# Placing the weighing of a tile behind the next tile's choice, and feeding the input patterns one tile earlier, in a four-layer graph and feed-forward kernel

## The chip, the cores and the metric

The kernel runs on one core of one Trainium2 chip, as one launch. The metric is the device time of a run in microseconds (us), from its start to its end; lower is better. The profiler's span of an execution is nearly that time (1441.6 us of 1443.37 us here).

## The reference

Four layers work on 1250 tokens of width 512, in fp32: a three-step graph network, a mixture of 16 experts with three chosen per token, a graph layer with attention and batch normalization, and the layer that this case is about, with the residual x added to each:

```
h           = layernorm(x)                                    # 1250 x 512
input_acts  = gelu(h @ input_patterns.T)                      # 1250 x 256
proc        = gelu(input_acts @ process_input_weights.T)      # 1250 x 1024
top, idx    = top_k(proc, 128)
agg         = softmax(top) @ process_values[idx]              # 1250 x 256
output_acts = gelu(agg @ output_input_weights.T)              # 1250 x 256
x           = x + output_acts @ output_patterns
```

So each token keeps the 128 largest of its 1024 process activations, weighs them by a softmax, and mixes the values with these weights.

## The kernel before

The 1250 tokens are ten tiles of 125 (`NT = 10`). Every engine has one program with its instructions in fixed order. Semaphores order the engines against each other, and an instruction that waits holds everything behind it on its engine. The layers before the last one are not touched by the diff.

**Inputs of the last layer.** VectorE normalizes tile i (line 449), TensorE turns it with four transposes (`pe_turn`, line 454) into one of two banks, and ScalarE copies it to SBUF (`act_turned`, line 460, which raises `hT_in`). `pe_inputs(c, f)` multiplies the pair of tiles 2c and 2c+1 with half f of the input patterns: eight records of 250 columns at line 426. It waits until both tiles of its pair are copied. There are five pairs and two halves, so ten such groups. In the loop, the group for pair and half `divmod(i - 2, 2)` follows the turn of tile i, so the turn of one more tile stands between a pair's last turn and its first group. Behind the loop stand the two groups of the last pair. ScalarE then loads its Gelu table and evicts six pieces (line 1015), and TensorE begins the process products when all six are there.

**The choice.** A threshold per token is refined by counts, so that a little over or just under 128 values stay above it. GpSimd marks what lies below the threshold (line 734) and leaves the rest in `rest` (line 736). For tile i it does so when tile i-2 is chosen (`bad_ready`). VectorE then finds the exact cut in `vec_choose(i)`: eight largest of the rest (line 1285), replace them (lines 1286 and 1289), the next eight (line 1292), a small subtraction (line 1297), and small instructions on 16 or 1 columns (lines 1300 to 1309), whose last raises `bad_ready`. TensorE adds up the flags of `bad` over the partitions (line 2264) and ScalarE stores the sum as an integer (line 810, which raises `bad_in`).

**The weighing.** `vec_weigh(i)` waits for that integer and for the exponentials, reads the integer into a register (`value_load`, line 1315), branches, and in the usual branch does one `scalar_tensor_tensor` over 1024 columns with two SBUF inputs (line 1327), which keeps the exponentials of the chosen values and sums them. Its end raises `weighed`. A reciprocal of the sum follows (line 1330, raising `w_inv_ready`). TensorE turns the weights with eight transposes (line 2249), ScalarE copies them, TensorE multiplies them with the values in 16 records (line 426), ScalarE applies Gelu, and TensorE multiplies with the output patterns. VectorE adds the result to x (line 1757), and SyncE stores it.

**The order of the last loop.** The choices of tiles 0 and 1 (`EARLY = 2`) and their weighings stand ahead of it, between the refinements. In the loop over t from 2 to 14, VectorE first adds the finished tile t-5 and then makes the choice of tile t. The weighing of tile t-1 is called inside that choice, right behind line 1292. Tile 9's weighing stands behind the add of tile 5. TensorE's iteration t turns the weights of tile t-3, turns the outputs of t-4, sums the flags of t-2, multiplies the patterns of t-5 and the values of t-3, in this order.

Of the kernel before, what the change touches and what calls it, by code (L numbers as in the profile page):

```python
# [17 lines left out]
NT = N_TOK // TP  # L18
# [3 lines left out]
IN_PAIRS = 5  # L22
# [40 lines left out]
EARLY, EARLY_FROM, CHOICE_PARTS = 2, 5, 4  # L63
# [17 lines left out]
def build(nc, a):  # L81
    with ExitStack() as ctx:
# [3 lines left out]
        def sem(name):  # L86
            return ctx.enter_context(nc.semaphore(name))
# [176 lines left out]
        def expert_views(slot):  # L264
# [150 lines left out]
        weighed, w_inv_ready, w_turned, wT_in, pv_mm, pv_in = (  # L415
            sem(n) for n in ("weighed", "w_inv_ready", "w_turned", "wT_in", "pv_mm", "pv_in"))
# [7 lines left out]
        def group(e, out, pairs):  # L424
            for n, (l, r) in enumerate(pairs):
                ins = e.matmul(out, l, r, start=(n == 0), stop=(n == len(pairs) - 1))  # L426
            return ins
# [56 lines left out]
        def of_tiles(t, s, first=0, last=NT):  # L484

            return [first + t - s] if 0 <= t - s < last - first else []
# [790 lines left out]
            e.wait_ge(v_own, v.n)  # L1277
            e.scalar_tensor_tensor(thr[:, c], left[:, c], step[:, c], thr[:, c], ALU.mult, ALU.add).then_inc(done, 1)

        def vec_choose(e, i, part, weigh=None):  # L1280

            c, r = slice(i, i + 1), rest[:, i % 2, :]
            if part == 0:
                e.wait_ge(chosen_pool, BELOW + 2 * i + 1)
                e.max(cand[:, i, 1:9], r).then_inc(v_own, v.up())
                e.tensor_copy(cand[:, i, 0:1], thr[:, c]).then_inc(v_own, v.up())
                e.wait_ge(v_own, v.n)
            elif part == 1:
                e.match_replace(r, cand[:, i, 1:9], r, REPLACED).then_inc(v_own, v.up())
                e.wait_ge(v_own, v.n)  # L1290
            elif part == 2:
                e.max(cand[:, i, 9:17], r).then_inc(v_own, v.up())

                if weigh is not None:
                    vec_weigh(e, weigh)
                e.wait_ge(counted_c, i + 1)
                e.tensor_scalar(left[:, c], cnt[:, c], float(K_PROC - N_PROC), None, ALU.add).then_inc(v_own, v.up())
                e.wait_ge(v_own, v.n)
            else:
                e.scalar_tensor_tensor(cut_junk, iota16, left[:, c], cand[:, i, 0:16], ALU.is_equal, ALU.mult,  # L1300
                                       accum_out=cut[:, c]).then_inc(v_own, v.up())
                e.wait_ge(v_own, v.n)
                e.tensor_scalar(cut_junk, cand[:, i, 1:17], cut[:, c], None, ALU.is_ge, ALU.add,
                                accum_out=cut_cnt[:, c]).then_inc(v_own, v.up())
                e.tensor_scalar(bad[:, c], cut[:, c], 0.0, None, ALU.is_le).then_inc(v_own, v.up())
                e.wait_ge(v_own, v.n)
                e.tensor_tensor(cut_cnt[:, c], cut_cnt[:, c], left[:, c], ALU.not_equal).then_inc(v_own, v.up())
                e.wait_ge(v_own, v.n)
                e.tensor_tensor(bad[:, c], bad[:, c], cut_cnt[:, c], ALU.add).then_inc(bad_ready, 1)

        def vec_weigh(e, i):
            r, w = junk[:, 1, :], wexp[i % 3]
            e.wait_ge(bad_in, i + 1)
            e.wait_ge(exp_ready, i + 1)
            failed = e.value_load(bad_i[0:1, i:i + 1], min_val=0, max_val=2 * TP)
            with e.If(failed > 0):
                src = acts[:, i, :]
                for n in range(K_PROC // 8):
                    e.max(top_s, src)
                    e.drain()  # L1320
                    e.match_replace(r, top_s, src, REPLACED)
                    e.drain()
                    src = r
                e.scalar_tensor_tensor(w, r, REPLACED, w, ALU.is_equal, ALU.mult,
                                       accum_out=w_sum[:, i:i + 1]).then_inc(weighed, 1)
            with e.Else():
                e.scalar_tensor_tensor(w, acts[:, i, :], cut[:, i:i + 1], w, ALU.is_ge, ALU.mult,
                                       accum_out=w_sum[:, i:i + 1]).then_inc(weighed, 1)
            e.wait_ge(weighed, i + 1)
            e.reciprocal(w_inv[:, i:i + 1], w_sum[:, i:i + 1]).then_inc(w_inv_ready, 1)  # L1330
# [13 lines left out]
        def vector(e):  # L1344
# [409 lines left out]
            for t in range(EARLY, NT + 5):  # L1754
                for i in of_tiles(t, 5):
                    e.wait_ge(pat_mm, i + 1)
                    e.tensor_tensor(x_res[:, i, :], x_res[:, i, :], psum[0:TP, 6 + i % 2, :], ALU.add).then_inc(x_last, 1)
                for i in of_tiles(t, 0):
                    for part in range(CHOICE_PARTS):
                        vec_choose(e, i, part, i - 1 if i > EARLY else None)  # L1760
                if t == NT:
                    vec_weigh(e, NT - 1)


        def pe_z(e, l, i, w, b):
# [145 lines left out]
        def pe_busy(e, b, operand, n, rows=128):  # L1911

            for _ in range(n):
                e.matmul(psum[0:rows, b, :], ident[0:rows, 0:rows], operand, start=True, stop=True)  # L1914
# [10 lines left out]
        def pe_inputs(e, c, f):  # L1925

            if c == 0 and f == 0:
                e.wait_ge(ld_last, 16)
                e.wait_ge(pv_in, 4)
            e.wait_ge(hT_in, 5 * NT + 2 * c + 2)  # L1930
            o = c * 2 * TP
            ins = group(e, psum[:, 2 + c // 2 * 2 + f, c % 2 * 2 * TP:(c % 2 + 1) * 2 * TP],
                        [(w_ip[:, k, f * 128:(f + 1) * 128], hT[:, k, o:o + 2 * TP]) for k in range(KD)])
            if c % 2 == 1 or c == IN_PAIRS - 1:
                ins.then_inc(ia_mm, 1)
# [38 lines left out]
        def tensor(e):  # L1974
# [244 lines left out]
            for i in range(NT):  # L2219
                e.wait_ge(ln_out, 3 * NT + i + 1)  # L2220
                if i >= 2:
                    e.wait_ge(hT_in, 5 * NT + i - 1)
                pe_turn(e, htok[:, i, :], i % 2)
                if i >= 2:
                    pe_inputs(e, *divmod(i - 2, 2))
            for f in range(2):
                pe_inputs(e, IN_PAIRS - 1, f)


            for i in range(NT):  # L2230
# [9 lines left out]
            e.wait_ge(pv_in, 4)  # L2240
            for t in range(EARLY, NT + 5):
                for i in of_tiles(t, 3):
                    e.wait_ge(weighed, i + 1)
                    for g in range(2):
                        if i >= 1:
                            e.wait_ge(wT_in, 2 * (i - 1) + g + 1)
                        for k in range(4):
                            c = (4 * g + k) * 128
                            ins = e.transpose(psum[:, 1 + g, k * TP:(k + 1) * TP], wexp[i % 3][:, c:c + 128],
                                              ident[0:TP, 0:TP])  # L2250
                        ins.then_inc(w_turned, 1)
                if t == EARLY + 1:
                    pe_busy(e, 7, w_op[:, 0, :], 2)
                for i in of_tiles(t, 4):
                    e.wait_ge(o_in, i + 1)
                    e.wait_ge(outT_in, i)
                    for k in range(2):
                        ins = e.transpose(psum[:, 4, k * TP:(k + 1) * TP], o_act[:, i % 2, k * 128:(k + 1) * 128],
                                          ident[0:TP, 0:TP])
                    ins.then_inc(o_turned, 1)  # L2260
                for i in of_tiles(t, 2):
                    e.wait_ge(bad_ready, i + 1)
                    e.wait_ge(bad_in, i)
                    e.matmul(psum[0:1, 0, 0:1], ones_col, bad[:, i:i + 1], start=True, stop=True).then_inc(bad_mm, 1)
                if t == EARLY:
                    pe_busy(e, 7, w_op[:, 0, :], 6)

                for i in of_tiles(t, 5):
                    e.wait_ge(outT_in, i + 1)
                    if i >= 2:  # L2270
                        e.wait_ge(x_last, i - 1)
                    group(e, psum[0:TP, 6 + i % 2, :], [(outT[:, i % 2, k, :], w_op[:, k, :])
                                                        for k in range(2)]).then_inc(pat_mm, 1)
                for i in of_tiles(t, 3):
                    e.wait_ge(wT_in, 2 * i + 2)
                    e.wait_ge(o_in, i)
                    group(e, psum[0:TP, 3, 0:D_PV], [(wT[:, i % 2, k, :], w_po[:, k, :])
                                                     for k in range(8)]).then_inc(o_mm, 1)
# [60 lines left out]
```

## Time and profile before

| what | value |
|---|---|
| median of three runs | 1439.91 us (1437.83 to 1443.37) |
| the profiled execution, its own time | 1443.37 us |
| its span | 1441.6 us |
| TensorE matmuls busy | 1311.9 us, 91% |
| VectorE busy | 582.5 us, 40% |
| ScalarE busy | 467.7 us, 32% |
| GpSimd busy | 206.5 us, 14% |
| chain that ended last | PE 76%, DVE 9%, DMA 6%, ACT 3% |

PE is TensorE, DVE is VectorE, ACT is ScalarE, POOL is GpSimd; an engine's name with a q is its sequencer, which runs waits, register loads and branches. The shares are of the whole span. The diff touches two short stages: from about 1280 to 1308 us (normalization and input patterns) and from about 1366 us to the end (choices, weighings, values). So what counts is the order of instructions in these two stretches. Times in the rows are in us from the start of the span.

### The profile page before, as it was taken

To read this page: it belongs to the slowest core of one execution; us is meant where nothing else is said; L and a number is where in the kernel's file an instruction comes from. 1 tells how busy PE (TensorE), PEld (TensorE's weight loads), DVE (VectorE), ACT (ScalarE), POOL (GpSimd) and SP (SyncE) were. 2 spreads that over 40 slices of the span, in tenths; PEclk is the share of its full clock that TensorE was granted. 3 is DMA by queue.
4 is the path that set the end of the run, shared out by engine and by line. 5 is a ranking of instruction groups with operands and counts; after the bars stand their busy time and mean duration, and the time that the engine had idled before them with its cause. 6 is when DMAs were issued, how large, how long until landed. Compare 5 with 4: busy or idle time off the path is not lost.

```text
span 1441.6 us, 18234 instructions
## 1 busy us (share of the span) xinstructions
PE 1311.9 (91%) x5780; PEld 832.3 (58%) x5781; DVE 582.5 (40%) x1558; ACT 467.7 (32%) x1004; POOL 206.5 (14%) x207
## 2 busy tenths in 40 slices
PE   4899999999999899899898999898479999999787
PEld 2454485566466454377575776665355577565465
DVE  9999822111144351111111111111275334675894
ACT  5799632222122200011111111111122333327883
POOL 1000000000000046000101111101383000022361
PEclk9999999999999899999999999999879989999899
DMA  9100000000111214241156115244352000100001
GB/s 219 60 1 1 2 1 0 2 1 1 47 56 33 99 24 148 94 136 44 63 187 217 44 44 207 94 160 167 110 160 94 1 30 1 67 0 1 0 24 50
DMA packets 45297, 96.92 MB, mean 67 GB/s; under 512 B 8495, under 2 KB 10857, under 8 KB 44065
## 3 DMA queue, kind: packets, MB, share of 16 engines
q1 hardware_dynamic: 27205, 68.70, 14.2%
q0 software_dynamic: 10560, 16.23, 4.2%
q10 hardware_dynamic: 7452, 10.97, 2.1%
q8 instruction: 45, 0.74, 0.2%
q14 instruction: 35, 0.29, 0.1%
HBM read 79.72 MB, written 16.10 MB: 66 GB/s over the span
## 4 chain that ended last, share of the span: by engine, by line
PE 76%; DVE 9%; DMA 6%; ACT 3%; issue 3%; ACTq 1%; POOL 1%; DVEq 1%; SPq 0%; POOLq 0%
PE psum L426 38%; PE psum L1802 13%; PE psum L1857 7%; PE psum L1782 4%; PE psum L1997 3%; DMA sb_w_reg<-w_gnn 2%; DMA slot_outs<-sb_blk 2%; PE psum L1914 2%; PE psum L454 2%; PE psum L1940 1%; PE psum L1882 1%; ACT sb_htok L799 1%; DMA sb_blk<-rows,sb_blk 1%; PE psum L1832 1%; PE psum L2212 1%
## 5 line engine op out<-in xcount | busy, mean ns | idle before, releaser
L426 PE MATMUL psum<-sb_w_reg,sb_blk 128*128 128x256 f32 x896 | 206.2, 384 | 1.0 <-issue 1.0
L426 PEld LDWEIGHTS psum<-sb_w_reg,sb_blk 128*128 128x128 f32 x896 | 169.8, 193 | 33.3 <-issue 12.1
L1802 PE MATMUL psum<-sb_z_reg_r,sb_hT_conv_r 125*125 125x512 f32 x400 | 170.9, 427 | 0.2 <-issue 0.2
L426 PE MATMUL psum<-sb_w_reg,sb_hT_conv 128*125 128x512 f32 (+1 forms) x376 | 167.2, 594 | 0.0
L1802 PE MATMUL psum<-sb_htok_r,sb_hT_conv_r 125*125 125x512 f32 x300 | 118.8, 396 | 0.0
L1190 DVE TENSOR_TENSOR sb_blk<-sb_blk,psum 128x256 f32<-128x256 f32 x56 | 23.6, 422 | 221.5 <-ACT sb_blk L773 221.5
L426 PEld LDWEIGHTS psum<-sb_w_reg,sb_hT_conv 128*125 128x125 f32 (+1 forms) x376 | 68.4, 188 | 76.5 <-issue 75.8
L1857 PE MATMUL psum<-sb_w_reg,sb_blk 128*128 128x512 f32 x224 | 108.2, 605 | 2.2
L426 PE MATMUL psum<-sb_hT_conv,sb_w_reg 128*128 128x416 f32 (+3 forms) x336 | 104.7, 469 | 0.0
L752 ACT CAST sb_hT_conv_r<-sb_a_reg 125x625 fp32r<-125x625 f32 x80 | 56.1, 715 | 116.6 <-PE psum L1802 116.5
L1802 PEld LDWEIGHTS psum<-sb_z_reg_r,sb_hT_conv_r 125*125 125x125 f32 x400 | 76.0, 190 | 25.2 <-issue 7.6
L1997 PE MATMUL psum<-sb_hT_conv,sb_sil 125*125 125x400 bf16 x316 | 74.7, 364 | 13.5 <-DVE sb_a_reg L1405 5.3
L426 PEld LDWEIGHTS psum<-sb_hT_conv,sb_w_reg 128*128 128x128 f32 x336 | 64.8, 196 | 35.8 <-issue 32.0
L1397 DVE TENSOR_SCALAR sb_hT_conv<-sb_sil,sb_blk 125x400 bf16<-125x400 f16 x316 | 84.4, 370 | 0.0
L1782 PE MATMUL psum<-sb_w_reg,sb_hT_conv 128*125 128x512 f32 x160 | 81.4, 600 | 3.3 <-DMA sb_w_reg<-w_gnn 3.3
L1997 PEld LDWEIGHTS psum<-sb_hT_conv,sb_sil 125*125 125x125 bf16 x316 | 43.7, 143 | 67.9 <-DVE sb_a_reg L1405 34.9
L862 ACT ACTIVATE sb_blk<-sb_sil,sb_blk 125x125 bf16<-125x125 f16 x237 | 77.2, 391 | 7.1 <-DVE sb_blk L1359 5.6
L773 ACT ACTIVATE sb_blk<-psum 128x256 f32<-128x256 f32 x56 | 21.5, 383 | 168.3 <-PE psum L426 164.3
L426 PE MATMUL psum<-sb_w_reg,sb_z_reg 128*125 128x512 f32 x160 | 69.4, 594 | 1.3 <-ACT sb_z_reg L1015 0.7
L663 POOL IOTA sb_blk<- 125x160 f32 x1 | 0.3, 307 | 465.9 <-DVE sb_blk L1101 465.9
L1802 PEld LDWEIGHTS psum<-sb_htok_r,sb_hT_conv_r 125*125 125x125 f32 x300 | 56.3, 188 | 17.4 <-issue 4.8
L1857 PEld LDWEIGHTS psum<-sb_w_reg,sb_blk 128*128 128x128 f32 x224 | 40.2, 189 | 37.1 <-issue 26.8
(383 smaller groups left out, 1835.9 us busy)
## 6 DMA issues: line engine op xcount, KB each, us to landing
sb_hT_conv<-w_expert SPq DMA_DIRECT2D x7, 2048.0 KB, 11.2
sb_w_reg<-w_expert SPq DMA_DIRECT2D x6, 2048.0 KB, 9.6
sb_hT_conv<-w_expert SPq DMA_DIRECT2D x7, 1024.0 KB, 13.3
slot_outs<-sb_blk ACTq DMA_DIRECT2D x28, 256.0 KB
sb_w_reg<-w_expert SPq DMA_DIRECT2D x6, 1024.0 KB, 12.2
sb_w_reg<-w_gnn SPq DMA_DIRECT2D x1, 4096.0 KB, 44.8
sb_w_reg<-w_qkv SPq DMA_DIRECT2D x1, 3072.0 KB, 18.8
slot_outs<-sb_blk ACTq DMA_DIRECT2D x1, 2560.0 KB, 10.5
```

Of the source, the lines that this page charges most:

```text
L426: ins = e.matmul(out, l, r, start=(n == 0), stop=(n == len(pairs) - 1))
L454: ins = e.transpose(psum[:, b, k * TP:(k + 1) * TP], src[:, k * 128:(k + 1) * 128], ident[0:TP, 0:TP])
L752: e.copy(counts_at(l, n), adj[:, h * HALF_T:(h + 1) * HALF_T, tile(i)]).then_inc(counts_in, 1)
L773: e.activation(silg[:, h, :], psum[:, 1 + h, 0:HF], ACT.Silu).then_inc(s_sil, 1)
L862: e.activation(sq_lo[t % 2][:, j, :], neg_iota, ACT.Square, bias=neg_lo[:, c:c + 1], scale=-1.0).then_inc(lo_squared, 1)
L1190: e.tensor_tensor(hid[:, h * HF:(h + 1) * HF], silg[:, h, :], psum[:, 1 + h, HF:2 * HF], ALU.mult).then_inc(s_hid, 1)
L1397: e.tensor_scalar(hot_key[n][:, j, :], key_iota, key[:, c:c + 1], None, ALU.is_equal).then_inc(hot_ready, 1)
L1782: ins = e.matmul(psum[0:TP, bank, :], hT[:, k, tile(i)], w_gnn[:, 0 if own else 1, k, :], start=(k == 0), stop=(k == KD - 1))
L1802: ins = e.matmul(psum[0:TP, b, :], counts_at(l, 2 * i + n // NT)[:, s % HALF_T, :], z[s], start=(n == 0), stop=(n == len(pairs) - 1))
L1857: ins = e.matmul(psum[:, 5, :], hidT[:, k, :], w_dn[:, k, :], start=(k == 0), stop=(k == KD - 1))
L1914: e.matmul(psum[0:rows, b, :], ident[0:rows, 0:rows], operand, start=True, stop=True)
L1997: ins = e.matmul(psum[0:TP, t % 3, 0:KEYS], hot_lo[n][:, j, :], hot_key[n][:, j, :], start=(j == 0), stop=(j == RUN - 1))
```

## The change

Three edits. In `vec_choose` the call of `vec_weigh` behind line 1292 is taken out, and the last loop calls `vec_weigh(t-1)` behind the whole of `vec_choose(t)`; tile 9's weighing comes at t = 10 in both kernels, behind the add of tile 5. On TensorE, the turning of tile i's weights waits for `w_inv_ready` (the reciprocal) where it waited for `weighed` (the sum). And `pe_inputs` moves up by one tile: the group `divmod(i - 1, 2)` follows the turn of tile i, and one group is left behind the loop where there were two.

```diff
-        def vec_choose(e, i, part, weigh=None):
+        def vec_choose(e, i, part):
...
             elif part == 2:
                 e.max(cand[:, i, 9:17], r).then_inc(v_own, v.up())
-
-                if weigh is not None:
-                    vec_weigh(e, weigh)
                 e.wait_ge(counted_c, i + 1)
...
                 for i in of_tiles(t, 0):
                     for part in range(CHOICE_PARTS):
-                        vec_choose(e, i, part, i - 1 if i > EARLY else None)
-                if t == NT:
-                    vec_weigh(e, NT - 1)
+                        vec_choose(e, i, part)
+                if t > EARLY:
+                    for i in of_tiles(t, 1):
+                        vec_weigh(e, i)
...
                 pe_turn(e, htok[:, i, :], i % 2)
-                if i >= 2:
-                    pe_inputs(e, *divmod(i - 2, 2))
-            for f in range(2):
-                pe_inputs(e, IN_PAIRS - 1, f)
+                if i >= 1:
+                    pe_inputs(e, *divmod(i - 1, 2))
+            pe_inputs(e, IN_PAIRS - 1, 1)
...
                 for i in of_tiles(t, 3):
-                    e.wait_ge(weighed, i + 1)
+                    e.wait_ge(w_inv_ready, i + 1)
```

## Rows read from the trace of the kernel before

**Rows 1.** Timeline of VectorE, last loop: start, us, line, operation, shapes, idle before.

```profile
1363.76 1.23 DVE L1292 MAX8 sb_blk<-sb_htok 125x8 f32<-125x1024 f32 x1
1364.91 0.14 DVE L1297 TENSOR_SCALAR sb_blk<-sb_blk 125x1 f32<-125x1 f32 x1
1365.08 0.24 DVE L1300 SCALAR_TENSOR_TENSOR sb_blk<-sb_blk 125x16 f32<-125x16 f32 x1
...
1365.97 1.22 DVE L1285 MAX8 sb_blk<-sb_htok 125x8 f32<-125x1024 f32 x1
...
1368.60 1.23 DVE L1292 MAX8 sb_blk<-sb_htok 125x8 f32<-125x1024 f32 x1
1369.87 2.53 DVE L1327 SCALAR_TENSOR_TENSOR sb_htok<-sb_a_reg,sb_blk,sb_htok 125x1024 f32<-125x1024 f32 x1
...
1381.19 0.68 DVE L1757 TENSOR_TENSOR sb_x_res<-sb_x_res,psum 125x512 f32<-125x512 f32 x1
1381.79 1.22 DVE L1285 MAX8 sb_blk<-sb_htok 125x8 f32<-125x1024 f32 x1
...
1416.29 1.28 DVE L1327 SCALAR_TENSOR_TENSOR sb_htok<-sb_a_reg,sb_blk,sb_htok 125x1024 f32<-125x1024 f32 x1 [0.19 <-issue]
...
1417.69 0.14 DVE L1297 TENSOR_SCALAR sb_blk<-sb_blk 125x1 f32<-125x1 f32 x1
```

**Rows 2.** Timeline of GpSimd, the two instructions per tile, and an earlier one.

```profile
1342.99 2.84 POOL L734 TENSOR_SCALAR sb_hT_conv<-sb_a_reg,sb_blk 125x1024 bf16<-125x1024 f32 x1 [14.86 <-DVE sb_blk L1309]
...
1366.25 2.84 POOL L734 TENSOR_SCALAR sb_hT_conv<-sb_a_reg,sb_blk 125x1024 bf16<-125x1024 f32 x1 [3.21 <-DVE sb_blk L1309]
1369.17 2.14 POOL L736 TENSOR_TENSOR sb_htok<-sb_hT_conv,sb_a_reg 125x1024 f32<-125x1024 bf16 x1
```

**Rows 3.** Timeline of TensorE at the end of the last loop.

```profile
1410.52 1.07 PE L2249 MATMUL psum<-sb_ident,sb_a_reg 125*128 125x125 f32 x8 [0.80 <-DVE sb_a_reg L1327]
...
1417.63 1.07 PE L2249 MATMUL psum<-sb_ident,sb_htok 125*128 125x125 f32 x8 [0.30 <-DVE sb_htok L1327]
```

**Rows 4.** Chain that ended last, in order of time: start, us, what.

```profile
1358.89 0.31 DVEq L1315
...
1359.74 1.30 DVE sb_a_reg L1327 x2
...
1384.50 0.51 DVEq L1315
...
1385.88 1.75 DVE sb_a_reg L1327 x2
```

**Rows 5.** Timeline of VectorE, a small two-input instruction during GpSimd's line 734.

```profile
1343.21 0.90 DVE L1278 SCALAR_TENSOR_TENSOR sb_blk<-sb_blk 125x1 f32<-125x1 f32 x1
```

**Rows 6.** Timeline of TensorE, turns (L454) and input groups (L426).

```profile
1285.89 3.04 PE L426 MATMUL psum<-sb_hT_conv,sb_w_reg 128*128 128x250 f32 x8
1288.77 0.59 PE L454 MATMUL psum<-sb_ident,sb_htok 125*128 125x125 f32 x4
1289.20 1.85 PE L426 MATMUL psum<-sb_hT_conv,sb_w_reg 128*128 128x250 f32 x8
...
1301.53 0.59 PE L454 MATMUL psum<-sb_ident,sb_htok 125*128 125x125 f32 x4
1301.96 5.23 PE L426 MATMUL psum<-sb_hT_conv,sb_w_reg 128*128 128x250 f32 x24
```

**Rows 7.** Timeline of ScalarE: copy of tile 1, then the Gelu part.

```profile
1283.05 0.58 ACT L460 COPY sb_hT_conv<-psum 128x500 f32<-128x500 f32 x1 [1.15 <-PE psum L454]
...
1302.75 1.28 ACT L1015 ACT_TABLE_LOAD   x1
1304.05 2.30 ACT L1015 ACTIVATE sb_z_reg<-psum 128x500 f32<-128x500 f32 x5
1307.22 0.38 ACT L1015 ACTIVATE sb_z_reg<-psum 128x250 f32<-128x250 f32 x1 [0.88 <-PE psum L426]
```

**Rows 8.** Table by windows, TensorE: stretch, its length, busy (count), granted clock, DMA share, GB/s.

```profile
1286.00:1288.00 2.00, 2.00 (x7) 0.50 0.00 0
```

## The prediction

> **What bounds the kernel now.** I read first the page's shares and then only the two stretches that the diff touches: the chain of waits from 1280 us on, and the timelines of VectorE, GpSimd, TensorE and ScalarE beside it.
>
> In the last loop the chain lies on VectorE. TensorE waits 0.80 us per tile for line 1327 [rows 3], so it has about 6.8 us of work in a tile's period. That period is 15.22 / 2 = 7.61 us: the place behind tile 2's choice is at 1365.97 and that behind tile 4's at 1381.19 [rows 1]. I call this place, where the instruction behind line 1309 can start, the marker M of a tile. From M of tile 2 to the turning of tile 8's weights at 1417.63 [rows 1, 3] are 51.66 us. There the chain passes to TensorE, which works through the last tiles.
>
> The period is not VectorE's work alone. The weighing's instruction takes 1.28 us when it is free and 2.53 us in tile 2 [rows 1]. GpSimd's line 736 ran from 1369.17 to 1371.31 [rows 2], and the weighing that had begun at 1369.87 ended at 1372.40, which is 1.09 us behind it. So the weighing is held by a GpSimd instruction that the previous choice has started, and the loop closes over GpSimd.
>
> Before the weighing stand the register load and the branch. From the load's start to line 1327 are 0.85 us in one tile and 1.38 us in another [rows 4]. Nearly all of it lies under line 1292, which runs 1.15 us until the next instruction when nothing is between (1363.76 to 1364.91) [rows 1].
>
> **The change part by part.**
>
> *A choice without the weighing inside.* Line 1285 to line 1292 is 2.63 us (1365.97 to 1368.60), line 1292 to line 1297 is 1.15 us, line 1297 to M is 1.06 us: 4.84 us. The add of a finished tile puts 0.60 us ahead (1381.19 to 1381.79) [rows 1].
>
> *The weighing behind it.* The load can now start at about M, and nothing long runs on VectorE meanwhile: the cover is gone. The trace bounds the way to line 1327 with 0.85 and 1.38 us; I take 1.1, near the middle. Line 1327 and its reciprocal take 1.40 us to the next instruction (1416.29 to 1417.69) [rows 1], so 2.50 us.
>
> *What GpSimd does meanwhile.* Line 734 starts 0.28 us behind M (1366.25 against 1365.97) [rows 1, 2]. It holds two-input instructions of VectorE for a part of its run: a one-column instruction begun at 1343.21 ended at 1344.11, which is 1.12 us behind line 734's start at 1342.99 and 1.72 us before its end [rows 2, 5]. I take 1.10 us for the hold itself. The weighing then ends 0.28 + 1.10 + 1.09 = 2.47 us behind M, and the next instruction starts at 2.59: hardly later than 2.50. Line 736 comes at M + 3.20 and now finds no two-input instruction, so the stall that the old order had is gone. That gain is counted by the sum.
>
> The Trainium skill puts it otherwise (SBUF — State Buffer, "Who interferes with whom"): the shared port pair is locked for the whole instruction. By that rule the weighing would wait out line 734, which is the second rival below. The trace disagrees, with 0.90 us where the rule wants about 2.6.
>
> *The sum from M of tile 2.* Tile 3's choice has no weighing ahead of it, but its line 1300 would start at 3.95 us (2.63 + 1.15 + 0.17), in line 736, which ends 5.34 us behind M (1371.31). It ends with that, and 0.65 us later is M of tile 3: 6.01 us. Tile 4: weighing 2.59 and choice 4.84, 7.43. Tiles 5 to 8 with an add: 8.03 each, 32.12. Tile 9, with no line 734 behind tile 8's choice: 2.50 + 0.60 + 4.84 = 7.94. Then the weighing of tile 8: 1.1 us, 1.34 us from line 1327's start to the turning (1416.29 to 1417.63) [rows 1, 3], and about 0.2 us for the reciprocal, which TensorE now waits for too: 2.64. Together 56.14 us against 51.66: **+4.5 us**. The later wait costs that 0.2 us once; in the middle tiles TensorE has slack, and tile 9's weights are ready long before TensorE reaches them. The bounds: all weighings free of GpSimd at 0.85 us would give +2.3; all at 1.38 us would give +6.0.
>
> What is queued behind? GpSimd's next tile, ScalarE's exponential and count, and the flag's way back each have over 2 us before VectorE wants them, because they are started by M or by the weighing of a tile before, and the period has grown. The tail from 1417.63 on keeps its length.
>
> *Input groups one tile earlier.* In the steady run a turn and a group take 2.13 us (six pairs from 1288.77 to 1301.53), 0.43 for the turn and 1.69 to 1.70 for the group [rows 6]. Today a turn of another tile covers the copy on ScalarE. In the new order the first group of a pair stands right behind the turn of its second tile. The copy of tile 9 ended at 1302.75, 1.22 us behind its turn's start [rows 6, 7]; with 0.04 us to the matmul, TensorE waits until 1.25, where the turn itself needs 0.43. It loses 0.82 us at each of tiles 3, 5, 7 and 9: 3.28 us. It wins the start: the first group needs only tiles 0 and 1, copied at 1283.63 [rows 7], and not 1285.89. If the clock holds, the groups end at 1283.67 + 10 x 1.69 + 8 x 0.43 + 3.28 = 1307.29, against 1307.19 (1301.96 + 5.23) [rows 6]. ScalarE is then the later one: tile 9's turn starts at 1302.66, its copy ends at 1303.88, and the table (1.30) and five Gelus (2.30) end at 1307.48, so that the sixth starts there and not at 1307.22 [rows 7]: **+0.3 us**.
>
> The clock matters here. The first group ran at 0.50 of the full clock, that is at 1.2 GHz [rows 8], and took 2.88 us to the next turn, not 1.69 [rows 6], after TensorE had done little but two short turns. In the new order the first group itself fills that idle time, so I expect 2.4 GHz to last. If it falls anyway, the 1.19 us are paid and this part costs +1.4.
>
> Sum: +4.5 + 0.3 = **+4.8 us**. Against the profiled execution's 1443.37 us that is 1448.2. That execution was the slowest of the three runs, 3.5 us over the median; so against the median of 1439.9 it is **1444.7 us**, 0.33% slower. I count a change of more than 0.5%, about 7.2 us, as what a measurement of this kernel can tell from none.
>
> **The rivals.**
>
> *The clock falls in the input stage too.* The sum is +5.9, 1445.8 us. For it: TensorE now has four waits of 0.82 us. Against it: a wait of 0.80 us stands in the last loop too [rows 3], and the eight transposes behind it took 1.07 us, no more than those behind 0.30 us.
>
> *GpSimd's line 734 holds the weighing to its end.* The place is tiles 2 to 6, five weighings, each 2.84 - 1.10 = 1.74 us later: +8.7, in all +13.5, 1453.4 us, slower. It decides from the point where the hold lasts about 0.5 us longer than 1.10, since five times that passes the 7.2 us. For it: line 736 held the weighing to its end. Against it: the row of 0.90 us [rows 5]. It is a one-column instruction, so I don't rule the rival out.
>
> *The sequencer hides the branch.* If the load and branch run ahead under the small instructions, line 1327 starts at M. The weighing costs 1.40: 6.01 + 6.24 + 5 x 6.84 + 1.54 = 47.99, which is -3.7, and -3.4 with the inputs: 1436.5 us. TensorE's 6.8 us would just allow it. Against it: the load stands behind line 1309 in one queue, and line 1309 waits for its predecessor.
>
> *TensorE becomes the bound in the last loop.* Its waits grow from 0.80 to about 1.2 us per tile, and up to 3 us once before tile 2's turning. If that keeps its clock down for much of a period, 6.8 us grow past 8.03 and the tail slows as well; with the one slow group as a measure (1.19 us lost in 1.69) two of these per tile in five tiles give +12 less the wait of 1.2 in each: +6, in all about +11, 1450.7 us.
>
> **How the numbers follow.** Forecast 0.64, slow clock in the input stage 0.14, hold to the end 0.08, TensorE as the bound 0.07, hidden branch 0.07. The likeliest gives 1444.7; its own range by the bounds of the branch is +2.6 to +6.3, 1442.5 to 1446.2, and with the scatter of the median (the runs shown span 5.5 us) 1440.5 to 1449. The full range reaches down to 1439.5 and up to 1452, which leaves the hold rival and most of the hidden branch out, about 0.15. Slower by over 0.5% is 0.08 + 0.07 and a tenth from the first two by scatter: 0.24. Faster by over 0.5% would take 1432.7 and has only scatter and a mechanism I don't see: 0.03. Within 0.5%: 0.73.
>
> **What would show it.** Right: a spacing of line 1285's starts of about 8.0 us in tiles 5 to 8; line 1327 at 1.1 to 1.4 us behind M with a length under 1.6 us and idle time named issue or its sequencer ahead of it; no line 1327 stretched by line 736; line 1300 of tile 3 alone stretched to about 1.4 us; TensorE's first input group near 1283.7 at full clock, and waits of 0.8 us on line 460. Wrong: lengths of line 1327 near 3 us (the hold), a period set by TensorE without idle time there, or a period under 7.6 us. A branch that costs far more than 1.38 us without its cover would break the sum upward.

## The result and the profile after

The changed kernel takes 1447.0 us (median of 10 runs, 1444.0 to 1452.9), the kernel before 1439.0 us in the same comparison. The ratio is 1.0054, with a 95% interval of 1.0037 to 1.0073: slower, by 5.3 to 10.5 us. It lies astride the 0.5% that the prediction took as the bound of what can be told. The profiled execution's span is 1449.9 us, where that of before was 1441.6 us.

Of these 8.3 us, 2.15 arose ahead of the change: tile 0's turn in the last layer begins at 1282.59 us, and in the kernel before at 1280.44 us, and no instruction up to there differs. So I measure both traces from that turn. M is the marker of the prediction, the place behind a choice's last instruction.

| stretch | before | after | difference |
|---|---|---|---|
| tile 0's turn to the end of the sixth Gelu of the inputs | 27.16 us | 29.60 us | +2.44 |
| from there to M of tile 2 | 58.37 | 58.18 | -0.19 |
| from there to the turning of tile 8's weights | 51.66 | 55.84 | +4.18 |
| from there to the span's end | 23.97 | 23.69 | -0.28 |
| sum | 161.16 | 167.31 | +6.15 |

(The starts are those of the timelines. M is the start of line 1306's instruction, line 1309 before, plus 0.08 us.)

**The input stage.** The timeline of TensorE after the change answers to [rows 6]:

```profile
1284.52 0.65 PE L454 MATMUL psum<-sb_ident,sb_htok 125*128 125x125 f32 x4 [1.28 <-DVE sb_htok L449]
1285.93 3.47 PE L426 MATMUL psum<-sb_hT_conv,sb_w_reg 128*128 128x250 f32 x8 [0.76 <-ACT sb_hT_conv L460]
1289.23 0.59 PE L454 MATMUL psum<-sb_ident,sb_htok 125*128 125x125 f32 x4
1289.66 1.85 PE L426 MATMUL psum<-sb_hT_conv,sb_w_reg 128*128 128x250 f32 x8
1291.36 0.59 PE L454 MATMUL psum<-sb_ident,sb_htok 125*128 125x125 f32 x4
1292.62 1.95 PE L426 MATMUL psum<-sb_hT_conv,sb_w_reg 128*128 128x250 f32 x8 [0.67 <-ACT sb_hT_conv L460]
1294.41 0.59 PE L454 MATMUL psum<-sb_ident,sb_htok 125*128 125x125 f32 x4
```

The first group begins behind tile 1's turn, as the edit says, but takes 3.30 us to the next turn (1285.93 to 1289.23), nearly twice the 1.70 us of the next group. The windows of TensorE show why. A row gives the stretch, its length, the busy time (with the count), the granted clock as a share of 2.4 GHz, and the DMA share and rate:

```profile
1284.00:1286.00 2.00, 0.72 (x5) 0.91 0.00 0
1286.00:1288.00 2.00, 2.00 (x5) 0.50 0.00 0
```

The clock fell to 1.2 GHz about 0.3 us ahead of the group (0.91 over the first window is a fall at some 1285.6). Each later pair has a wait named line 460, the copy on ScalarE: from tile 3's turn at 1291.36 to tile 4's at 1294.41 are 3.05 us, where a turn with its group had 2.13.

**The last loop.** The timeline of VectorE answers to [rows 1]; its rows are a late instruction of tile 3's choice, tile 2's weighing, the end of tile 5's choice, tile 4's weighing, the add of a finished tile, and the end of tile 6's choice:

```profile
1374.31 1.43 DVE L1297 SCALAR_TENSOR_TENSOR sb_blk<-sb_blk 125x16 f32<-125x16 f32 x1
...
1377.23 1.63 DVE L1324 SCALAR_TENSOR_TENSOR sb_htok<-sb_a_reg,sb_blk,sb_htok 125x1024 f32<-125x1024 f32 x1 [0.76 <-issue]
...
1391.77 0.16 DVE L1306 TENSOR_TENSOR sb_blk<-sb_blk 125x1 f32<-125x1 f32 x1
1393.03 1.28 DVE L1324 SCALAR_TENSOR_TENSOR sb_a_reg<-sb_a_reg,sb_blk 125x1024 f32<-125x1024 f32 x1 [1.10 <-issue]
...
1394.44 0.67 DVE L1754 TENSOR_TENSOR sb_x_res<-sb_x_res,psum 125x512 f32<-125x512 f32 x1
...
1399.78 0.16 DVE L1306 TENSOR_TENSOR sb_blk<-sb_blk 125x1 f32<-125x1 f32 x1
```

Line 1306 ends a choice, and line 1324 is the weighing. It starts 1.18 us behind the marker at 1391.85, and VectorE is idle for 1.10 us ahead of it. From one line 1306 to the next are 8.01 us. The chain that ended last shows what fills the idle time: the register load (line 1312) and the branch (line 1313) on VectorE's sequencer. From tile 2's weighing to tile 8's they are on it in every tile, with nothing of VectorE running over them:

```profile
1391.85 0.31 DVEq L1312
...
1392.20 0.18 DVEq L1312
...
1392.48 0.07 DVEq L1313
1392.55 0.48 issue
1393.03 1.30 DVE sb_a_reg L1324 x2
```

And GpSimd's instructions beside these two weighings, answering to [rows 2]:

```profile
1376.67 2.84 POOL L734 TENSOR_SCALAR sb_hT_conv<-sb_a_reg,sb_blk 125x1024 bf16<-125x1024 f32 x1 [0.96 <-DVE sb_blk L1306]
...
1392.12 2.84 POOL L734 TENSOR_SCALAR sb_hT_conv<-sb_a_reg,sb_blk 125x1024 bf16<-125x1024 f32 x1 [2.97 <-DVE sb_blk L1306]
1395.05 2.15 POOL L736 TENSOR_TENSOR sb_htok<-sb_hT_conv,sb_a_reg 125x1024 f32<-125x1024 bf16 x1
```

Line 734 begins at 1392.12 and does not end before 1394.96, but the weighing that starts at 1393.03 inside it takes its free 1.28 us. Tile 2's weighing, which started 0.56 us behind line 734 (1377.23 against 1376.67), took 1.63. The others took 1.28 to 1.33. Line 1297 in tile 3's choice took 1.43 us in place of 0.24, under line 736. Line 736, which held the weighing in [rows 1], now finds nothing to hold. TensorE, last, answers to [rows 3]:

```profile
1394.58 1.07 PE L2246 MATMUL psum<-sb_ident,sb_a_reg 125*128 125x125 f32 x8 [1.24 <-DVE sb_blk L1327]
...
1426.21 1.07 PE L2246 MATMUL psum<-sb_ident,sb_htok 125*128 125x125 f32 x8 [1.18 <-DVE sb_blk L1327]
```

In a middle tile it waits 1.24 us where it waited 0.80, and for the reciprocal (line 1327 here).

### The profile page after: what moved, and what is told of

It is laid out like the page before. It is cut to its first block, busy times and chain, and to the rows that moved or that the text cites. A ratio compares the mean times of both kernels' runs of the same rounds, so it can differ in the third digit from the quotient of the medians.

```text
span 1449.9 us, 18234 instructions
## 1 busy us (share of the span) xinstructions
PE 1309.9 (90%) x5780; PEld 830.2 (57%) x5781; DVE 579.3 (40%) x1558; ACT 467.4 (32%) x1004; POOL 206.3 (14%) x207
## 4 chain that ended last, share of the span: by engine, by line
PE 74%; DVE 12%; DMA 4%; ACT 3%; issue 3%; ACTq 1%; POOL 1%; DVEq 1%; POOLq 0%
PE psum L426 38%; PE psum L1800 13%; PE psum L1855 7%; PE psum L1780 4%; PE psum L1995 3%; DMA slot_outs<-sb_blk 3%; PE psum L454 1%; PE psum L1938 1%; DVE sb_hT_conv L1394 1%; PE psum L1880 1%; DMA sb_blk<-rows,sb_blk 1%; PE psum L1912 1%; PE psum L1830 1%; ACT sb_htok L799 1%; DVE sb_htok L1289 1%
## 5 line engine op out<-in xcount | busy, mean ns | idle before, releaser
L426 PE MATMUL psum<-sb_w_reg,sb_blk 128*128 128x256 f32 x896 | 206.8, 384 | 0.7 <-issue 0.7
L426 PEld LDWEIGHTS psum<-sb_w_reg,sb_blk 128*128 128x128 f32 x896 | 170.2, 193 | 33.0 <-issue 11.6
L426 PE MATMUL psum<-sb_w_reg,sb_hT_conv 128*125 128x512 f32 (+1 forms) x376 | 167.2, 594 | 0.0
L426 PEld LDWEIGHTS psum<-sb_w_reg,sb_hT_conv 128*125 128x125 f32 (+1 forms) x376 | 68.4, 188 | 76.5 <-issue 75.9
L426 PE MATMUL psum<-sb_hT_conv,sb_w_reg 128*128 128x416 f32 (+3 forms) x336 | 102.5, 461 | 3.4 <-ACT sb_hT_conv L460 3.4
L426 PEld LDWEIGHTS psum<-sb_hT_conv,sb_w_reg 128*128 128x128 f32 x336 | 63.4, 192 | 38.6 <-issue 31.7
L1394 DVE TENSOR_SCALAR sb_hT_conv<-sb_sil,sb_blk 125x400 bf16<-125x400 f16 x316 | 80.4, 319 | 0.0
L426 PE MATMUL psum<-sb_w_reg,sb_z_reg 128*125 128x512 f32 x160 | 69.4, 594 | 1.3 <-ACT sb_z_reg L1015 0.7
```

The costliest lines, as they stand in the source:

```text
L1394: e.tensor_scalar(hot_key[n][:, j, :], key_iota, key[:, c:c + 1], None, ALU.is_equal).then_inc(hot_ready, 1)
```

## The experiments

The whole time of this kernel scatters: in one comparison 35 runs of the kernel before span 1433.7 to 1453.2 us. Over the profiled executions of the experiments tile 0's turn begins between 1272.0 and 1285.5 us with the same work ahead of it. A few us are therefore read from the traces, by the stretches of the table above. Each kernel has one trace, so the stretches need a measure of their own: where the instructions are the same, the loop repeats to 0.01 us (51.66 and 51.65; 55.84, 55.83 and 55.83), while the old order's input stage comes out in two lengths 1 us apart, and the stretch to M of tile 2 in two lengths about 2.4 us apart. The last section says why. Here are all kernels. "Spacing" is from M to M for tiles 5 to 8. A kernel without a ratio was run once, for its trace.

| kernel | turn to sixth Gelu | to M of tile 2 | to tile 8's turning | to the end | sum | spacing | ratio to before (95%) |
|---|---|---|---|---|---|---|---|
| before | 27.16 | 58.37 | 51.66 | 23.97 | 161.16 | 7.61 | |
| after | 29.60 | 58.18 | 55.84 | 23.69 | 167.31 | 8.02 | 1.0054 (1.0037 to 1.0073) |
| e1_inputs_only | 29.52 | 58.14 | 51.65 | 24.12 | 163.43 | 7.61 | 1.0010 (0.9989 to 1.0031) |
| e2_weigh_only | 26.18 | 58.06 | 55.83 | 23.97 | 164.04 | 8.02 | 1.0004 (0.9976 to 1.0032) |
| e3_after_no_branch | 29.50 | 57.28 | 48.94 | 24.01 | 159.73 | 6.91 | 0.9996 (0.9968 to 1.0023) |
| e4_pool_early | 27.10 | 60.04 | 51.72 | 24.02 | 162.88 | 6.90 to 9.85 | 0.9977 (0.9951 to 1.0003) |
| e5_wait_only | 27.03 | 58.31 | 51.89 | 24.00 | 161.23 | 7.62 | |
| e6_weigh_in_part0 | 27.25 | 60.57 | 45.98 | 24.36 | 158.16 | 6.69 to 6.88 | 0.9967 (0.9949 to 0.9985) |
| e7_before_no_branch | 26.18 | 57.22 | 51.39 | 24.08 | 158.87 | 7.62 | |
| e8_filled_gap | 28.04 | 60.59 | 55.83 | 24.02 | 168.48 | 8.02 | 1.0039 (1.0019 to 1.0058) |
| e9_part0_filled | 26.19 | 57.04 | 45.98 | 24.44 | 153.65 | 6.69 to 6.87 | 0.9958 (0.9939 to 0.9977) |
| e10_load_early | 29.73 | 60.57 | 54.36 | 23.80 | 168.46 | 8.01 | |

### The two halves of the change

**e1_inputs_only** has the input edit alone.

```diff
-                if i >= 2:
-                    pe_inputs(e, *divmod(i - 2, 2))
-            for f in range(2):
-                pe_inputs(e, IN_PAIRS - 1, f)
+                if i >= 1:
+                    pe_inputs(e, *divmod(i - 1, 2))
+            pe_inputs(e, IN_PAIRS - 1, 1)
```

> The kernel before with the input groups one tile earlier, nothing else. Theory of the prediction's parts as the trace after shows them: the first group starts about 0.1 us behind tile 1's copy and runs at 1.2 GHz (3.3 us where 1.69 us at 2.4 GHz), and four restarts behind a copy cost 0.92 us each; so the last Gelu of the six ends about 2.4 us later than in the kernel before, counted from tile 0's turn, and the run is 2.3 us (0.16%) slower, last loop unchanged with 7.61 us per tile. Rival: the later stages take the shift up (their slack hides it), below 0.5 us in all. Second rival: the stretch is rigid and some of the 8 us of the whole change comes from here: over 4 us.

The input stage takes 29.52 us, 2.36 more than in the kernel before, and everything behind it keeps its length: 163.43 against 161.16, +2.3 us. The shift is passed on whole. The timed ratio of +0.1% agrees with that 0.16%, and with no change as well.

**e2_weigh_only** is the changed kernel with the input groups put back (the diff above, the other way).

> The changed kernel with the input groups put back; the weighing behind the choice and the wait for the reciprocal stay. Theory (uncovered load and branch): 8.01 us per tile, 55.8 us from tile 2's marker to the turning of tile 8's weights where the kernel before has 51.7, so +4.2 us (0.29%). Rival: the parts don't add up, and this part alone gives the whole 8 us or, with the other order of inputs, under 2 us.

The last loop is that of the changed kernel, 55.83 us, +4.2. So the parts add up stretch by stretch. The timed ratio, +0.04%, is below the +0.3% of the stretch, which lies at the upper end of its interval, and the timed ratios of e1 and e2 together give +0.14% where the whole change has +0.54%: the adding up is shown by the traces and not by the times. The input stage took 26.18 us in this execution, 1 us less than in the kernel before with the same instructions: the clock did not fall here, and the first group ran at full speed.

**e5_wait_only** changes only what the turning waits for.

```diff
-                    e.wait_ge(weighed, i + 1)
+                    e.wait_ge(w_inv_ready, i + 1)
```

> The kernel before with TensorE's wait for the reciprocal in place of the sum, nothing else. Theory: 0.2 us, once, at the turning of tile 8's weights, and no change in the spacing of 7.61 us; from tile 2's marker to that turning 51.8 to 51.9 us. Rival: the later start of TensorE in each tile is passed on (flag, exponentials, counts) and the spacing grows by 0.2 us, 1.2 us in all.

51.89 us against 51.66, with the spacing unchanged: 0.2 us, once.

### What the later weighing costs

**e3_after_no_branch** is the changed kernel without the load and the branch. The fallback for tokens whose cut failed is left out.

```diff
-            failed = e.value_load(bad_i[0:1, i:i + 1], min_val=0, max_val=2 * TP)
-            with e.If(failed > 0):
...
-            with e.Else():
-                e.scalar_tensor_tensor(w, acts[:, i, :], cut[:, i:i + 1], w, ALU.is_ge, ALU.mult,
-                                       accum_out=w_sum[:, i:i + 1]).then_inc(weighed, 1)
+            e.scalar_tensor_tensor(w, acts[:, i, :], cut[:, i:i + 1], w, ALU.is_ge, ALU.mult,
+                                   accum_out=w_sum[:, i:i + 1]).then_inc(weighed, 1)
```

> The changed kernel without the register load and the branch: the usual path's weighing is always done, the fallback for tokens with a failed cut is left out. Theory (the uncovered load and branch are the cost): line 1324's counterpart starts at the marker, 1.2 us earlier per tile, nothing holds it, 6.8 us per tile, about 8 to 9 us less than the changed kernel and so about 1 to 2 us less than the kernel before. Rival (GpSimd's marking instruction holds the weighing): it still ends 2.2 us behind that instruction's start, 8.0 us per tile, no gain.

The spacing falls from 8.02 to 6.91 us. The timeline of VectorE around one weighing (line 1312 here):

```profile
1379.21 0.16 DVE L1306 TENSOR_TENSOR sb_blk<-sb_blk 125x1 f32<-125x1 f32 x1
1379.29 1.28 DVE L1312 SCALAR_TENSOR_TENSOR sb_a_reg<-sb_a_reg,sb_blk 125x1024 f32<-125x1024 f32 x1
...
1392.14 0.32 DVE L1297 SCALAR_TENSOR_TENSOR sb_blk<-sb_blk 125x16 f32<-125x16 f32 x1
```

The weighing begins at the marker. Now it is ahead of GpSimd's line 734, and that one is the one that waits, 3.72 us where it took 2.84:

```profile
1379.57 3.72 POOL L734 TENSOR_SCALAR sb_hT_conv<-sb_a_reg,sb_blk 125x1024 bf16<-125x1024 f32 x1 [0.96 <-DVE sb_blk L1306]
...
1390.28 2.14 POOL L736 TENSOR_TENSOR sb_htok<-sb_hT_conv,sb_a_reg 125x1024 f32<-125x1024 bf16 x1
```

The 6.91 us are GpSimd's again, by a little: line 736 ends at 1392.42, and line 1297 of that choice is held to 1392.46, 0.32 us where it takes 0.23.

**e7_before_no_branch** takes the same lines out of the kernel before.

> The kernel before without the register load and the branch (the fallback path is left out). Theory: in the old order the load and branch are covered by line 1292 and the weighing's end is set by GpSimd's line 736, so tiles 3 to 8 keep 7.61 us each and the way from tile 2's marker to the turning of tile 8's weights stays at 51.7 us, within 0.4 us. Rival: the load and branch cost the same in either order, as they did 1.1 us per tile in the new one; then 6.5 to 6.9 us per tile.

The same edit that won 1.1 us per tile in the new order wins nothing in the old one: 7.62 us, and 51.39 us to tile 8's turning, 0.27 less. The weighing starts earlier and lasts longer, to the same end; in tile 2 it takes 2.66 us where [rows 1] has 2.53. So in the old order the branch was covered, and the weighing's end was GpSimd's to set. Outside the loop the edit does win: tile 1's weighing, which stands behind a whole choice in both orders, begins 1.89 us behind M of tile 1 and not 2.92, and M of tile 2 comes 1.15 us sooner (57.22 against 58.37).

**e10_load_early** moves only the load back under line 1292 in the changed kernel.

```diff
+        early_load = {}
+
+        def vec_load(e, i):
+            e.wait_ge(bad_in, i + 1)
+            early_load[i] = e.value_load(bad_i[0:1, i:i + 1], min_val=0, max_val=2 * TP)
...
                 e.max(cand[:, i, 9:17], r).then_inc(v_own, v.up())
+                if i > EARLY:
+                    vec_load(e, i - 1)
...
-            failed = e.value_load(bad_i[0:1, i:i + 1], min_val=0, max_val=2 * TP)
+            if i not in early_load:
+                vec_load(e, i)
+            failed = early_load[i]
```

> The changed kernel with the register load of tile i-1's flag moved back behind line 1292 of tile i's choice; the branch and the weighing stay behind the whole choice. Theory: the weighing can start 0.5 to 0.9 us behind the marker and not 1.2, but GpSimd's marking instruction holds it for its first 1.1 us, so it is stretched to 1.6 to 1.9 us, ends 2.45 to 2.5 us behind the marker in each of tiles 2 to 6, and the spacing stays near 8.0 us (7.95 to 8.0). Only tile 7's and 8's weighings, with no marking instruction beside them, win 0.4 us each. Rival (the hold costs nothing and the load is half of the uncovered cost): 7.5 us per tile and a length of 1.28 us throughout.

```profile
1381.01 0.16 DVE L1314 TENSOR_TENSOR sb_blk<-sb_blk 125x1 f32<-125x1 f32 x1
1381.68 1.87 DVE L1334 SCALAR_TENSOR_TENSOR sb_a_reg<-sb_a_reg,sb_blk 125x1024 f32<-125x1024 f32 x1 [0.51 <-issue]
```

```profile
1381.36 2.84 POOL L734 TENSOR_SCALAR sb_hT_conv<-sb_a_reg,sb_blk 125x1024 bf16<-125x1024 f32 x1 [0.97 <-ACT sb_htok L816]
```

The first fence is VectorE's timeline, the second GpSimd's. The weighing begins 0.59 us behind the marker (1381.09) and not 1.2, and still ends at 1383.55, 2.46 us behind it and 2.19 behind line 734's start. It was stretched to 1.87, 1.91, 1.95 and 1.94 us in tiles 3 to 6, and the spacing stays at 8.01. So a part of the hold is real, and it ends at just the place where the uncovered branch lets a weighing end: a weighing that begins behind line 734's start, from 0.6 to 1.2 us behind the marker in these traces, ends 2.46 us behind it. Only one that begins ahead of line 734 escapes, as in e3. Two details went another way. Tile 2's weighing began 0.21 us behind its marker, ahead of line 734, and was free; and of the two without line 734 beside them, tile 7's won more than 0.4 us: tile 9's M came 7.04 us behind tile 8's, where it was 7.66.

### What held the old loop

**e4_pool_early** is the kernel before, with GpSimd released by the end of line 1292.

```diff
+        rest_read = sem("rest_read")
...
-                    e.wait_ge(bad_ready, i - 1)
+                    e.wait_ge(rest_read, i - 1)
...
-                e.max(cand[:, i, 9:17], r).then_inc(v_own, v.up())
+                e.max(cand[:, i, 9:17], r).then_inc(rest_read, 1)
...
+                e.wait_ge(rest_read, i + 1)
                 e.wait_ge(v_own, v.n)
```

> The kernel before, with GpSimd's marking of tile i released by the end of line 1292 of tile i-2 (which has read the buffer) and not by the end of the whole choice, about 1.1 us earlier. Theory (in the kernel before, GpSimd's second instruction holds the weighing, so the loop closes over GpSimd): the hold ends 1.1 us earlier in each period, 6.9 to 7.1 us per tile, about 3.5 to 4.5 us faster (0.3%). Rival (the period is VectorE's own work and TensorE's): 7.6 us per tile, no gain.

Undecided in time (0.9977, up to 1.0003). In the trace the 3.5 to 4.5 us that were expected did not come: the loop takes 51.72 us, as before. The spacings are 6.84, 6.86, 9.85, 7.49, 7.29 and 6.90 us for tiles 3 to 8. In all tiles of the loop but one the weighing is free (1.28 us). In that one the collisions come back, and one of them on another instruction: a weighing of 2.15 us, and a one-column instruction of 1.91 us in the middle of a choice:

```profile
1377.55 2.15 DVE L1329 SCALAR_TENSOR_TENSOR sb_a_reg<-sb_a_reg,sb_blk 125x1024 f32<-125x1024 f32 x1 [0.23 <-issue]
...
1380.68 1.91 DVE L1309 TENSOR_TENSOR sb_blk<-sb_blk 125x1 f32<-125x1 f32 x1
```

The spacings below 7 us support that the hold by GpSimd made 7.61 us, and the others show that moving the holder is no cure. Why the median came out 3 us lower while the trace's sum is 1.7 us higher isn't explained; 1.7 us of that sum lie ahead of the loop, in a collision of tile 1's weighing (last section).

**e6_weigh_in_part0** moves the weighing the other way, to an earlier place in the next choice, behind lines 1285 and 1286.

```diff
                 e.tensor_copy(cand[:, i, 0:1], thr[:, c]).then_inc(v_own, v.up())
+                if weigh is not None:
+                    vec_weigh(e, weigh)
...
-                if weigh is not None:
-                    vec_weigh(e, weigh)
```

> The kernel before with the weighing of tile i-1 behind line 1285 of tile i's choice, where it stood behind line 1292; the load and the branch are then under line 1285, and the weighing is over or begun when GpSimd's line 736 starts. Theory: about 7.1 us per tile where the kernel before has 7.61, since neither the hold nor the branch is paid in full; 48 to 49 us from tile 2's marker to the turning of tile 8's weights, 3 us (0.2%) faster than before. Rival: the flag's way over TensorE and ScalarE (M + 1 us) comes too late here and TensorE, which sums the flag ahead of its products, waits for each choice: 7.6 us per tile or more, no gain.

Faster, 0.9967 with 0.9985 as the upper end. The spacing is 6.69 to 6.88 us, and tile 8's turning comes 45.98 us behind M of tile 2, 5.7 us less than before.

```profile
1389.46 1.22 DVE L1285 MAX8 sb_blk<-sb_htok 125x8 f32<-125x1024 f32 x1
1390.60 0.14 DVE L1286 COPY sb_blk<-sb_blk 125x1 f32<-125x1 f32 x1
1390.71 1.29 DVE L1327 SCALAR_TENSOR_TENSOR sb_htok<-sb_a_reg,sb_blk,sb_htok 125x1024 f32<-125x1024 f32 x1
```

Here the branch is covered by line 1285, and the weighing begins 1.57 us behind line 734's start (1389.14) and ends at 1392.00, 0.07 us ahead of line 736 (1392.07). It is free of both, the second by a narrow margin. The gain was more than the 3 us that were expected, because the 7.1 us per tile were too many: an add (0.60), a choice (4.84) and a free weighing with its reciprocal (1.40), all terms of the prediction, are 6.84.

### The clock in the input stage

**e8_filled_gap** is the changed kernel with two fill matmuls in TensorE's idle time.

```diff
                 pe_turn(e, htok[:, i, :], i % 2)
+                if i < 2:
+                    e.matmul(psum[:, 2, 0:512 - 256 * i], ident, w_o[:, 0, 0:512 - 256 * i], start=True, stop=True)
```

> The changed kernel with two fill matmuls of 512 and 256 columns into a free bank behind the turns of tiles 0 and 1, in TensorE's idle time. Theory (1.6 of the input stage's 2.4 us are the first group's lower clock): the granted clock stays at 1.00, the first group takes 1.7 us and not 3.3, and from tile 0's turn to the end of the sixth Gelu are about 1.4 to 1.6 us less than the 29.6 us of the changed kernel. Rival: the clock falls all the same, or VectorE's normalization then sets the pace: under 0.5 us less.

```profile
1288.14 1.93 PE L426 MATMUL psum<-sb_hT_conv,sb_w_reg 128*128 128x250 f32 x8 [0.32 <-ACT sb_hT_conv L460]
1289.91 0.59 PE L454 MATMUL psum<-sb_ident,sb_htok 125*128 125x125 f32 x4
```

The first group takes 1.77 us, the clock stays at 1.00, and the stage takes 28.04 us, 1.56 less than in the changed kernel. The gain is lost again in this execution: the stretch to M of tile 2 is 60.59 us, 2.4 more, by a collision at tile 1's weighing that the last section tells of. The timed ratio, 1.0039, can't be told from the changed kernel's 1.0054.

### A version that beats both

**e9_part0_filled** takes e6's order, tile 1's weighing into tile 2's choice as well, and one fill matmul behind the first two turns of the old input order.

```diff
+                if i < 2:
+                    e.matmul(psum[:, 2, :], ident, w_o[:, 0, :], start=True, stop=True)
...
-            vec_weigh(e, 1)
...
-                        vec_choose(e, i, part, i - 1 if i > EARLY else None)
+                        vec_choose(e, i, part, i - 1)
```

> The kernel before with three edits meant to gain: the weighing behind line 1285 of the next choice, tile 1's weighing in tile 2's choice too (so that VectorE no longer waits 2.8 us for tile 1's flag behind TensorE's fill matmuls), and one fill matmul behind the turns of tiles 0 and 1 in the input stage. Theory: 6.7 to 6.9 us per tile (45.5 to 46.5 us from tile 2's marker to the turning of tile 8's weights), 1.2 us less in the input stage, and 1.0 to 1.5 us less up to tile 2's marker, in all 7 to 9 us (0.5 to 0.6%) faster than the kernel before. Rival: TensorE is the bound from here on and the gains ahead of the loop only turn into idle time before its chain: 5 to 6 us, as the weighing's move alone.

0.9958 (0.9939 to 0.9977) against the kernel before, and 7.5 us less in its trace: 1.0 in the input stage, 1.3 up to M of tile 2, 5.7 in the loop, less 0.5 at the tail. The 1.0 us can't be given to the fill alone, since e2 and e7 had it without one. It stands against a ratio of 1.0054 for the changed kernel, but the two were not run in one comparison.

## Why the prediction was right, and where it was off

- **The time.** 1444.7 us was forecast, 4.8 slower; measured are 1447.0, with the median of before at 1439.0. The range held it, and the sign was right. But 1447.0 lies above the 1442.5 to 1446.2 that the prediction's mechanism allowed and is held only by what was added for scatter. "Within 0.5%" had most of the chance, 0.73, and the ratio came out at 0.54%, with its interval on both sides of that bound.
- **The weighing behind the choice.** The step was +4.5 us, 56.14 against 51.66. Measured: 55.84, +4.18. By its terms: tile 3 was 6.01 and is 6.03 us; tile 4 was 7.43 and is 7.41; tiles 5 to 8 were 8.03 each and are 8.04, 8.01, 8.02 and 8.01; tile 9 was 7.94 and is 7.66, because the load and branch took 0.83 us there (1415.89 to 1416.72) and not 1.1. e3 and e7 show the mechanism from both sides. One part of the match is luck: the 2.59 us from M to the instruction behind the weighing were set by the hold in the prediction, with the branch at 1.1. In the run the branch took 1.18 us, which gives 2.59 without any hold (1391.85 to 1394.44), and the hold showed only in tile 2 (1.63 us) and by 0.05 us in tiles 5 and 6.
- **GpSimd's hold.** Taken as 1.10 us from line 734's start and no longer. Shown by e10 and by tile 2's weighing, which ended at 1378.86, 2.19 us behind line 734's start at 1376.67. The rival of a hold to the end falls: the weighing at 1393.03 ran its free 1.28 us within line 734. The lock for the whole instruction that the Trainium skill states (SBUF — State Buffer, "Who interferes with whom") was not seen for this instruction; for line 736 the traces agree with it, 2.53 us in [rows 1].
- **The wait for the reciprocal.** 0.2 us once; e5 shows 0.23.
- **The input groups.** This step failed: +0.3 was forecast with the clock staying up, and the rival in which it falls came true, +2.4. The failed sentence is that the first group itself would fill the idle time. It did not keep the clock: in all four executions of this order without a fill (after, e1, e3, e10) it fell, between 0.4 us ahead of the group's start (e1, e3) and 0.9 us behind it (e10), and the stage took 29.5 to 29.7 us. That rival, too, was too small, 1.4 where 2.4 was measured, by two mis-sized terms and some small ones. The slow group cost 1.6 us (3.30 against 1.70) and not 1.19, which I had read from a group that was only partly slow. And each restart behind a copy costs 0.92 us (3.05 - 2.13) and not 0.82, since the first matmul of a group that follows a wait adds 0.1: four of them, 0.4 us. The last 0.2 or 0.3 us are a first group that began 0.15 us behind its copy and not 0.04, and the 0.16 us by which a group's last record outlasts the next start (1.85 against 1.69), which the sum for the end of the groups left out. e8 shows the clock's part: 1.56 us back. It also shows that the clock was not the whole fault of the step. With the clock up, the new order's stage takes 28.04 us (e8) and the old one's 26.18 or 26.19 (e2, e7, e9), so the new order costs 1.85 us even then. The kernel before, from which +0.3 was counted, had lost 1 us to the clock itself.
- **What is left.** The traces give +6.15 us from the first touched instruction on, and the runs 5.3 to 10.5. They agree. That the middle of the runs, 7.8, is above the traces' sum is not explained here, and the timed ratios of e1 and e2 are too wide to settle it. The collision of the last section, which costs about 2.4 us in some executions and was absent from both profiled ones here, could make such a difference; how often it comes in either kernel was not measured.

## What to carry to other kernels

A register load with a branch cost VectorE 0.8 to 1.2 us here unless a long instruction that was issued ahead of it still ran; place it behind such an instruction, and with the data at hand. Before moving a two-input VectorE instruction, lay GpSimd's timeline beside it: the period may be set by the collision and not by either engine's work, and then work can be taken out without gain, as in e7, or the same work can be moved by 2 to 3 us for a gain, as in e6. And where TensorE's next instruction needs ScalarE's copy of a turn, put one more independent turn between: without it each restart cost 0.92 us here.

## What was not expected

Tile 1's weighing, which the diff leaves alone, comes out in one of two ways. TensorE's fill matmuls of line 1914 (1912 after the change) stand ahead of tile 1's flag and run at the low clock for a time that differs by execution: 5.1 us of them in the kernel before and 6.1 in e8, by the granted clock of the windows. In the kernel before they took 7.93 us, and the weighing began at 1359.74, 0.29 us ahead of GpSimd's line 736 at 1360.03: it was free. In e8 they took 8.41 us, and this is VectorE's and then GpSimd's timeline:

```profile
1365.47 3.04 DVE L1324 SCALAR_TENSOR_TENSOR sb_a_reg<-sb_a_reg,sb_blk 125x1024 f32<-125x1024 f32 x1 [3.31 <-ACT sb_blk L810]
```

```profile
1365.28 2.15 POOL L736 TENSOR_TENSOR sb_htok<-sb_hT_conv,sb_a_reg 125x1024 f32<-125x1024 bf16 x1
```

It began 0.19 us behind line 736, was held for 1.76 us, and M of tile 2 came 2.4 us later (60.59 against 58.18 us). Half a microsecond of the clock's timing turns into 2.2 to 2.4 us in this way in e6, e8 and e10, with the changed order and with the old one. In e4, where GpSimd starts earlier, the same weighing took 2.01 us, and the stretch 60.04. e9, which takes this weighing into tile 2's choice, has it free, at 1.28 us; one execution doesn't show that it always will be.

The input stage has two outcomes as well. With the same instructions the old order took 27.0 to 27.3 us in four executions and 26.18 in two (e2 and e7), by whether the clock fell after the first turns.
